# One transformer layer on one core: each norm with its own chain of roots, and a new order of work for all engines

## The reference

```python
x: 8 x 1024 token ids; h = segm_table[2] + sinusoid_pos + token_table[x]   # 8 x 1024 x 192, f32
h = h + attn(layernorm(h))       # 12 heads of 16, q and k layer-normed per head, softmax over 1024 keys
h = h + ffn(layernorm(h))        # 192 -> 768 -> 192, quantised to integers -8..7, erf gelu
# attn: qkv = x @ Wqkv.T;  q = ln(q) * 16**-0.5;  k = ln(k);  out = softmax(q k^T) v;  out @ Wproj.T
# ffn:  xq = round(clip(x/a1)); gelu(xq @ wq1.T * aw1*a1 + b1); hq = round(clip(./a2)); hq @ wq2.T * aw2*a2 + b2
```

## Time and profile before

| | us |
|---|---|
| median of 3 runs (lowest, highest) | 1040.18 (1038.93, 1041.99) |
| the profiled execution | 1038.85 |
| its span, first to last instruction | 1036.9 |
| PE busy (mean granted clock 0.985) | 962.3 |
| ACT busy | 874.8 |
| DVE busy | 829.6 |
| POOL busy | 410.0 |

### The profile page before, as it was taken

One profiled execution on the slowest core, in us unless ns is written; L12 is line 12 of the kernel. 1 busy time (PEld: TensorE's weight loads), 2 busy tenths in 40 slices (PEclk: granted clock), 3 DMA queues, 4 the chain that ended last, 5 costly groups with the idle time before them and its releaser, 6 DMA issues.

```text
span 1036.9 us, 19403 instructions
## 1 busy us (share of the span) xinstructions
PE 962.3 (93%) x7571; PEld 388.9 (38%) x7571; DVE 829.6 (80%) x2196; ACT 874.8 (84%) x950; POOL 410.0 (40%) x345
## 2 busy tenths in 40 slices
PE   5589989999999999999999999999999999988885
PEld 4333433434343343344344343434334343423223
DVE  5978879798888979888888979888898978734537
ACT  2377779898989989898989989898989989899983
POOL 6555106154462716354361625455371623210200
PEclk9789999999999999999999999999999999999997
DMA  7611001111120201211110211211010110000000
GB/s 157 140 16 17 2 1 19 14 17 32 16 37 28 26 20 16 62 16 32 13 34 32 24 25 16 62 17 31 9 24 16 20 28 1 16 16 1 16 1 31
DMA packets 25760, 28.59 MB, mean 28 GB/s; under 512 B 5027, under 2 KB 22182, under 8 KB 25670
## 3 DMA queue, kind: packets, MB, share of 16 engines
q0 software_dynamic: 16896, 11.80, 9.8%
q1 hardware_dynamic: 8624, 15.55, 4.8%
q10 hardware_dynamic: 150, 0.01, 0.0%
HBM read 21.06 MB, written 6.29 MB: 26 GB/s over the span
## 4 chain that ended last, share of the span: by engine, by line
PE 74%; DVE 12%; ACT 11%; issue 2%; POOL 0%; DMA 0%; DVEq 0%
PE ps_o L1285 31%; PE ps_s L1266 17%; ACT probs L719 10%; PE ps_j L1322 5%; PE ps_j L1313 4%; PE ps_j L1330 4%; PE ps_j L1358 3%; PE ps_j L1373 3%; PE ps_j L1336 2%; DVE o_sb L894 2%; PE ps_j L1341 1%; PE ps_j L1346 1%; DVE sq L875 1%; DVE stack L881 1%; ACT gelu L713 1%
## 5 line engine op out<-in xcount | busy, mean ns | idle before, releaser
L719 ACT ACTIVATE probs<-ps_s 128x1024 f32<-128x1024 f32 x768 | 738.5, 1024 | 93.8 <-PE ps_s L1266 86.7
L1285 PE MATMUL ps_o<-probs,v_sb 128*32 128x512 f32 x3072 | 397.1, 603 | 2.6 <-DVE o_sb L894 2.5
L1266 PE MATMUL ps_s<-qT,kT 64*128 64x512 f16 x1536 | 266.0, 384 | 17.7 <-ACT probs L719 13.6
L1266 PEld LDWEIGHTS ps_s<-qT,kT 64*128 64x128 f16 x1536 | 66.1, 93 | 339.1 <-ACT probs L719 265.9
L613 POOL TENSOR_TENSOR sq<-qk 128x384 f32<-128x384 f32 x56 | 46.3, 826 | 334.0 <-DVE qk L931 333.8
L623 POOL TENSOR_TENSOR stack<-sq,stack 128x384 f16<-128x384 f32 x124 | 127.0, 1102 | 117.5 <-DVE stack L881 117.5
L1285 PEld LDWEIGHTS ps_o<-probs,v_sb 128*32 128x32 f32 x3072 | 65.8, 108 | 125.0 <-issue 104.1
L558 POOL DMA_INDIRECT h_all<-in_L_tok_token_table,idx x60 | 93.3, 1556 | 20.3 <-issue 14.3
L558 POOL DMA_INDIRECT h_all<-in_L_tok_segm_table,idx x56 | 87.7, 1566 | 15.2 <-issue 13.1
L917 DVE TENSOR_SCALAR hq<-gelu 128x512 bf16<-128x512 f32 x90 | 75.0, 833 | 3.1
L1322 PE MATMUL ps_j<-wh,partsT 128*128 128x384 f16 (+1 forms) x384 | 71.4, 296 | 2.6 <-DVE w2T L945 1.0
(11 more groups left out here) (201 smaller groups left out, 1073.1 us busy)
## 6 DMA issues: line engine op xcount, KB each, us to landing
out<-h_all SPq DMA_DIRECT2D x15, 384.0 KB, 2.3
h_all<-in_positions SPq DMA_DIRECT2D x7, 768.0 KB, 4.3
gelu<-in_L_ffn_w SPq DMA_DIRECT2D x2, 576.0 KB, 12.7
h_all<-in_L_tok_token_table,idx POOLq DMA_INDIRECT x60
h_all<-in_L_tok_segm_table,idx POOLq DMA_INDIRECT x56
probs<-in_L_attn_qkv_weight SPq DMA_DIRECT2D x2, 432.0 KB, 6.4
h_all<-in_positions SPq DMA_DIRECT2D x2, 384.0 KB, 7.6
o_nat<-in_L_ffn_alpha_a SPq DMA_DIRECT2D x1, 384.0 KB, 5.0
```

The source lines that it names most:

```text
L719: nc.scalar.activation(probs[:, u % PROBS, 2 * pair:2 * pair + 2], ps_s[:, 2 * pair:2 * pair + 2], ACT.Exp, scale=SCORE_SCALE).then_inc(ex ...
L1266: last = mm(ps_s[:, j], kT[rows, par, head // 2, m * P:(m + 1) * P], qT[rows, par, head // 2, nh * NQ:(nh + 1) * NQ], start=True, stop=True)
L1285: last = mm(ps_o[32 * j:32 * j + 2 * D, :], v_sb[:, par, m, (GH * group + j) * VE:(GH * group + j) * VE + 2 * D], probs[:, u % PROBS, j], ...
```

## The change

The function of the roots takes a norm (`which`), 4 columns, and has two words, `R0` for the first norm and `Q0` for the second. PLAN is written anew for all engines.

```diff
 PLAN = """
-s h o h s
-s F0 q0 F1 F2 s
-s F3 q1 G0 h s
-s G1 P0 H0 s
-s H1 s h W0
-s s h h W1
-s s q2 q3 l0 R0 Y0 W2
-s N0 h s W3
-s h m0 s A0 W4
-s h s h m1 N1 W5
-s s B0 I0
-s s A1 Y1 B1 X0 o p0 X1 r0 B2 r1 X2 x0 X3 g B3 r2 X4 r3 X5 h h
-s S0 L0 n0 s h h
-s s x1 h
-s L1 C0 n1 s o
-s h s h L2
-s s n2 h
-s E0 x2 D0 s h
-s s C1 D1
+s s h h
+s s o Y0 W0 F0 P0 F1
+s s R0 h h a0
+s s W1 F2 N0 Y1 G0
+s s h h
+s s h F3 W2 A0
+s s H0 G1
+s s N1 B0 W3 H1
+s s h q0 h q1 q2
+s s l0 W4 o h A1
+s s Q0 m0 h
+s B1 s r0
 s h s h
-s s L3 n3 E1 E2 D2 x3
-s h s
-s h s E3 D3
-s h x4 t0 x5 a0 s
+s s m1 B2 r1 C0 r2
+s s W5 B3 I0 q3 h X0 r3 g X1 S0
+s s X2 X3 n0 n1 X4 X5 h x0 h h C1 o p0
+s s h
+s L0 L1 D0 L2 s n2 E0
+s h s x1
+s h n3 s L3 D1 E1
+s D2 s h
+s E2 s h
+s t0 s h x2
+s x3 D3 E3 s x4 h x5
 """
@@
-            def norm_roots(s0):
-                lo = 0 if job_runs("P", s0) else 1
-                hi = 2 if job_runs("H", s0) else 1
-                if lo < hi:
-                    rsqrt(rn[:, lo:hi], vn[:, lo:hi], wn[:, lo:hi])
+            def norm_roots(which):
+                rsqrt(rn[:, which], vn[:, which], wn[:, which])
@@
-                elif kind == "R":
-                    norm_roots(s0)
+                elif kind == "R" and job_runs("P", s0):
+                    norm_roots(0)
+                elif kind == "Q" and job_runs("H", s0):
+                    norm_roots(1)
```

## The result

| | before | changed |
|---|---|---|
| median us (lowest to highest), 4 runs each | 1041.09 (1038.93 to 1042.37) | 1053.3 (1051.61 to 1056.29) |
| ratio, with its 95% interval | | 1.0126 (1.0109 to 1.0143) |
| the profiled execution; its span | 1038.85; 1036.9 | 1056.29; 1054.3 |

The forecast was 1034.4. The measured time lies on the side of rival 1 (1045.2) and beyond it, and beyond the range's end of 1046.

A forecast was written before the change was run, and what follows sets the result against it. PE was taken as the bound, ACT close behind. Steady half steps summed to 0.0 each, half step 1 to -2.0, 13 to -0.8, 14 and 15 to -3.0: -5.8 us, so 1034.4; 8 times in 10 within 1027 to 1046.

The forecast's parts named there:

- rival 1: DVE becomes the bound of the second half, at x0 and x1 beside L0 to L2: +0.9 a half step, 1045.2; chance 0.24.
- DVE's full half: From B3's copy to x5, DVE works without pause; POOL's subtractions make o2 0.4 us late: +0.3 a half step.
- Roots: Second chain of 11 instructions adds 2.2 us of DVE to a half step, fitting its idle time: costs nothing.
- Gelu: PE waits for ACT's gelus where X2 to X5 now stand in a row: +1.2 us a half step.
- Dense scores: PE waits for exponentials at s21, s24, s27 and s38: +0.6 us a half step.
- Tokens: Token gathers start about 1 us later, P0 comes 3 us earlier and may wait 0.75, covered at G0: +0.
- Changes of kind: PE's changes between scores, heads and whole-array jobs fall from 69 to 67 at 0.1 us each: -0.2 a half step.
- Old waits: PE's short waits in the old order's steady half step, for copies and exponentials, go: -1.9 us a half step.
- Half step 1: With the weight jobs W: PE's waits for o and a late w2T copy shrink, W5 waits anew: -2.0 us.
- 13 and 14: In 13, a0 at the front removes PE's 0.79 wait: -0.8; in 14, exponentials idle 3.6 us, not 5.1: -1.5.
- 15: Last half step, ACT the bound: its idle falls from 5.2 to 3.6 us, -1.5.

The follow-up runs named there:

- e8: Changed kernel with only p0 (the segment gathers) moved between q0 and q1 on GpSimd; ratio to before 0.996, typical half step 58.99 us.
- e3: Changed kernel with GpSimd's L0 and L1 computed for one head of twelve only; ratio to before 0.9947, typical half step 58.98 us.
- e1: Changed kernel with x0 moved on VectorE from before C1 and o2 to behind E0; ratio to before 1.0001, typical half step 59.45 us.
- e2: Changed kernel with one copy in place of the second norm's chain of roots; ratio to before 1.0117, typical half step 60.35 us.
- e7: Kernel before, order untouched, with two chains of roots one behind the other at the old place; ratio to before 1.0067, typical half step 59.27 us.
- e12: The same kernel as e8, measured again with more rounds; ratio to before 0.9956, median 1035.17 us.
- e4: Changed kernel with two of the three instructions of x4 and x5 left out; ratio to before 1.0124, typical half step 60.34 us.
- e11: Changed kernel with a0 put back at the end of GpSimd's list; ratio to before 1.0501, typical half step 64.3 us.
- e6: Changed kernel with x0 moved behind E0 and p0 moved between q0 and q1; ratio to before 0.9997, typical half step 59.35 us.
- e0: No run of this name appears in the text given; no change and no time are told for it.

## Why the prediction was wrong

**DVE's full half, the step that failed.** It booked 2.4 us (x0) and 1.6 us (x1) of loss to POOL, `o2` 0.4 late and +0.2 at its heads. The heads wait 1.57. Two things were off in it. The place: I set L0 and L1 on x0, behind the gathers; L0 begins under n1's casts. The amount ahead of `o2`: 2.4 was booked, 3.8 measured. With 2.4 `o2` is 0.4 late, so each tenth more is PE's. (In e8, where L0 is on time, the same two losses are 1.3 and 1.0, the booked sum.) The bounds in that step (2.5 to 3.0 for a pair shut out) hold the 2.8 of n1; what I did not allow was a loss of that size with L1's behind it, in front of the same copy. e3 takes the loss away, e8 and half step 13 lessen it to the booked size, and each returns some 1.36 us; e1 takes x0 out from between the loss and the copy.

**Rival 1** has the mechanism, but neither the place nor the price: it set the losses at x0 and x1, shared them between `o2` and Y0, and said +0.9 a half step. Y0 waits for nothing, all is at `o2`, and it is +1.5. By the rule of the Trainium skill, "SBUF — State Buffer", section "Who interferes with whom", whichever of the two issues first keeps the ports for its whole instruction and the other is blocked; I made that a rival at 0.24. The traces agree with the blocking: held casts end 0.2 us and held instructions of x 0.28 us behind the end of a subtraction. They do not show the order in the 3.2 us cast, whose record starts 0.59 us ahead of the subtraction's (POOL's spans are rough).

**Roots** at nothing: right (e2), and where the cover is short it costs 0.44 (e7).

**Gelu** +1.2: from start to start X waits 0.23, 0.37 and 0.23, the first score behind 0.33: 1.16. **Dense scores** +0.6: 0.23, 0.11, 0.15 and 0.12, or 0.61; the wait booked at s38 is not among them, it is hidden behind that for `o2` (e8 has it, 0.28). **Tokens** +0: P0 starts its statistics with 0.65 of idle on DVE, which its cover takes. All three as booked.

**Changes of kind**, -0.2, has the wrong sign. The count of 69 and 67 includes the jobs W, which run in half step 1 alone. Without them the words change kind 64 times in the old order and 66 in the new one, and the steady half steps of the two traces show the same. At 0.1 each that is +0.2; from start to start, PE's jobs other than X take 17.1 us a half step before and 17.3 in the changed kernel.

**Old waits**, -1.9: the waits named are gone. The sum with the measured terms is then +0.2 - 1.9 + 1.16 + 0.61 + 1.57 = +1.6, against 1.52. For e8, with its 0.28 at s38 and no wait for `o2`, it is +0.35, against 0.16. What remains, up to 0.2 us, lies within what adding waits to differences of starts can tell, and stays open.

**Half step 1**: -2.6 for -2.0, although the wait for `o2` is in it too (1.67); without that wait e8 has -3.9. **13 and 14**: -0.4 and -1.1 for -0.8 and -1.5. The 0.79 us wait of the earlier trace rows is gone, but by the starts of the exponentials it falls into half step 14, which began at 889.92. In 13 the old order had a wait that the prediction does not name,

```profile
889.49 0.39 PE L1266 MATMUL ps_s<-qT,kT 64*128 64x512 f16 x2 [1.42 <-DVE qT L933]
```

behind the two instructions that `a0` held there (1.93 each). It is gone as well, but 58.99 is the new order's own pace there, so little is left of the gain. In 14 the exponentials idle 4.6 us in place of 5.1, not 3.6:

```profile
L719 ACT ACTIVATE probs<-ps_s 128x1024 f32<-128x1024 f32 x49 | 46.7, 1024 | 4.6 <-PE ps_s L1265 4.5
```

**15**: 0.0 for -1.5. The 5.2 us taken for it was all of ACT's idle in the stretch; before its exponentials it idled 4.4 there, and 4.7 in the new order. That gain did not exist. So of the -5.8 booked outside the steady half steps -4.0 came.

The forecast fits the kernel in which L0 is on time: e12 measured 1035.2. That is partly luck, since half step 1 gives 3.9 there and a typical half step loses 0.16.

## What to carry to other kernels

When an order of work is rewritten, lay each two-input GpSimd instruction against VectorE's list at its true start, with its own queue (gathers too) worked out, and add up all losses between there and the next copy that TensorE waits for: the sum of VectorE's work said nothing here (e2, e4), what stood between the loss and the copy decided (e1). The cheapest cure was not less work but GpSimd in time: four gathers moved to where it idles turned +1.3% into -0.4%. And a move that looks free (a0, x0) is to be tried against its absence, since it may be what makes another move possible (e11) or be a new wait of its own (e1, e6). A count, too, is to be taken over the words that run in the stretch in question: the jobs W turned +0.2 into -0.2.

## What the runs showed of the hardware

A cast of 128x384 that takes 0.36 us alone took 3.2 beside GpSimd's pair of subtractions: more than the pair's own 2.38. With the same pair begun ahead of two casts, both casts took 1.96 (e8). In all these places a held cast ends 0.2 us behind the end of a subtraction, and a held instruction of x (0.5 us alone, 1.02 held) 0.28 us behind it. So the loss is the time until GpSimd's instruction is over; one VectorE instruction is as a rule held by one GpSimd instruction, and through two of them only where the first came directly behind a gather. Gathers alone cost VectorE little: n0's two casts, at 464.73 during one, took 0.69, and 0.63 in e8 without one. So one overlap costs DVE 1.0 to 2.8 us. The second chain's instructions on 128x4 take 0.163 us, as against 0.167 on 128x8: half the columns, nearly the same time. And at waits of 1.6 to 4.1 us TensorE's granted clock sometimes fell from 1.00 to 0.50 and sometimes did not: at the same wait of 2.4 us it fell in most half steps of e11 and not in 7 and 10, and a stretch like that from 439.3 to 442.7 cost 1.6 us.
